# A two-layer graph network on one core: group sums laid between half batches, and two buffers for ScalarE's pair of passes

## The reference

```
# layer 0
msg = x[src] @ W_msg.T + b_msg + edge_embed[type]
messages = segment_sum(msg, dst, 3125)
x = layernorm(x + gru_cell(messages, x))
# layer 1, a SAGE layer applied twice (relu between)
neigh = segment_sum(h[src], dst) / max(degree, 1)
h = h @ w_self + neigh @ w_neigh + b
x = layernorm(x + h)
```

## Time and profile before

| | us |
|---|---|
| three runs | 766.2, 764.7, 766.98; median 766.2 |
| profiled execution: its time | 764.69 |
| its span, first to last instruction | 762.9 |
| time around the span (difference) | 1.8 |
| counting stage, first one-hot to the last pass of TensorE | about 15 to 403.6 |

### The profile page before, as it was taken

One profiled execution on the slowest core, in us unless ns is written; L12 is line 12 of the kernel. 1 busy time (PEld: TensorE's weight loads), 2 busy tenths in 40 slices (PEclk: granted clock), 3 DMA queues, 4 the chain that ended last, 5 costly groups with the idle time before them and its releaser, 6 DMA issues.

```text
span 762.9 us, 14609 instructions
## 1 busy us (share of the span) xinstructions
PE 662.5 (87%) x3061; PEld 311.9 (41%) x3061; DVE 468.4 (61%) x1469; ACT 244.3 (32%) x486; POOL 171.0 (22%) x342
## 2 busy tenths in 40 slices
PE   2767899989888899888766999948999999999995
PEld 0222344434333343333222544413555456666663
DVE  7789999998888879999894357651010010034434
ACT  3044444332422235656664245531111221100000
POOL 2432333232222235445340012230100111100000
PEclk9879999999999999999998999989999999999998
DMA  5000000000000000000002011000100110211210
GB/s 155 1 1 0 1 1 1 0 1 0 1 0 1 0 1 1 0 1 0 0 0 81 16 28 55 16 30 29 42 25 17 41 41 29 87 43 43 69 31 16
DMA packets 29437, 17.32 MB, mean 23 GB/s; under 512 B 1841, under 2 KB 28223, under 8 KB 29400
## 3 DMA queue, kind: packets, MB, share of 16 engines
q1 hardware_dynamic: 29400, 16.82, 7.6%
HBM read 10.38 MB, written 6.44 MB: 22 GB/s over the span
## 4 chain that ended last, share of the span: by engine, by line
PE 64%; DVE 18%; issue 7%; DVEq 5%; ACT 2%; DMA 1%; SPq 0%; POOL 0%; ACTq 0%
PE PS L917 14%; PE PS L994 11%; PE PS L1232 11%; PE PS L873 10%; DVE S L619 10%; DVE D L613 3%; PE PS L1161 3%; PE PS L1055 2%; PE PS L1196 2%; DVEq L619 2%; PE PS L895 1%; PE PS L1150 1%; PE PS L1149 1%; PE PS L1028 1%; PE PS L1029 1%
## 5 line engine op out<-in xcount | busy, mean ns | idle before, releaser
L917 PE MATMUL PS<-S,D 128*128 128x449 bf16 x780 | 219.0, 368 | 53.8 <-DVE S L619 45.4
L619 DVE TENSOR_SCALAR S<-iota_h,src_col,src_w 128x440 bf16<-128x440 f16 x749 | 253.1, 399 | 0.2 <-issue 0.2
L472 POOL COPY S<-T 128x27 bf16 (+1 forms) x262 | 113.5, 434 | 236.4 <-PE PS L917 222.2
L917 PEld LDWEIGHTS PS<-S,D 128*128 128x128 bf16 x780 | 75.7, 97 | 193.6 <-DVE S L619 152.3
L1275 ACT ACTIVATE AT<-digits 128x1152 uint8 (+5 forms) x75 | 77.1, 1029 | 160.7 <-DVE digits L608 160.7
L613 DVE TENSOR_TENSOR D<-iota_t,dst 128x384 bf16<-128x384 f16 x260 | 93.8, 361 | 33.3 <-PE PS L917 32.1
L873 PE MATMUL PS<-AT,xp 128*128 128x512 bf16 x375 | 91.3, 379 | 0.0
L994 PE MATMUL PS<-AT,x1p 128*128 (+2 forms) x450 | 86.8, 353 | 0.0
L1232 PE MATMUL PS<-xp,AT 128*128 128x384 bf16 (+1 forms) x525 | 85.6, 326 | 0.0
L1232 PEld LDWEIGHTS PS<-xp,AT 128*128 (+2 forms) x525 | 51.5, 98 | 33.9 <-issue 0.3
L994 PEld LDWEIGHTS PS<-AT,x1p 128*128 128x128 bf16 x450 | 39.5, 99 | 44.0 <-issue 2.3
(11 more groups left out here) (167 smaller groups left out, 628.8 us busy)
## 6 DMA issues: line engine op xcount, KB each, us to landing
slot<-x_rows SPq DMA_DIRECT2D x12, 256.0 KB, 2.9
xstage<-x SPq DMA_DIRECT2D x6, 256.0 KB, 4.9
x_rows<-slot SPq DMA_DIRECT2D x6, 256.0 KB, 2.2
y_rows<-slot SPq DMA_DIRECT2D x6, 256.0 KB, 2.2
res_rows<-slot SPq DMA_DIRECT2D x6, 256.0 KB, 2.2
slot<-res_rows SPq DMA_DIRECT2D x6, 256.0 KB, 3.1
out_rows<-slot SPq DMA_DIRECT2D x6, 256.0 KB, 2.2
slot<-xT SPq DMA_DIRECT2D x3, 256.0 KB, 2.6
```

What stands on the lines that cost most here:

```text
L472: g.tensor_copy(S[:, where:where + V, SPAN:WIDE], T[:, :, ds(c0 + where, V)].rearrange("p k c -> p c k")).then_inc(sem("types_placed"), 1)
L619: v.tensor_scalar(S[:, u, 0:SPAN], iota_h[:, :], src_col[:, ds(c0 + u, 1)], src_w[:, ds(c0 + u, 1)], ALU.is_equal, ALU.mult).then_inc(sem( ...
L917: mm(PS[:, par, 0:WIDE], ring[:, u, :], S[:, u, 0:WIDE], start=opens and u == 0, stop=last).then_inc(sem("tiles_summed" if last else "item ...
```

## The change

The plan of group sums is laid out for single steps. A table LEAST gives a least number of batches for each tile; that many passes, less one, are written out instead of looped, and a piece of steps stands after each of them and between its two halves. With `single = LEAST[t] - 2` there are `2 * single + 3` pieces: 3 in the tiles 0 to 8, 5 in 9 to 15, 7 in 16 to 18, 9 in 19 to 22, 23 in 23 and 24. The plan now sums to 125. The buffer `apart` becomes two buffers inside AT (a part that is written last), chosen by the parity of the batch, and ScalarE's wait after its second pass goes away. Four small table instructions of GpSimd at the start become ten.

```diff
--- before.py
+++ after.py
@@ -28,12 +28,11 @@
 TAIL = E - FULL * P
 U = 6
 V = U // 2
-PIECES = 3
 WIDE_TILES = 21
-LEAST = 2
-LEAST_WIDE = 4
+LEAST_RUNS = ((0, 9, 2), (9, 16, 3), (16, 19, 4), (19, 23, 5), (23, 25, 12))
+LEAST = tuple(n for lo, hi, n in LEAST_RUNS for _ in range(lo, hi))
 BATCHES = -(-CHUNKS // U)
-assert BATCHES < 1 << 10 and LEAST * WIDE_TILES + LEAST_WIDE * (TILES - WIDE_TILES) < BATCHES
+assert BATCHES < 1 << 10 and sum(LEAST) < BATCHES and len(LEAST) == TILES
 LAG = 3
 DIVIDE = -(-(1 << 16) // U)
 assert all(n * DIVIDE >> 16 == n // U for n in range(CHUNKS + U)) and (CHUNKS + U) * DIVIDE < 1 << 24
@@ -60,7 +59,7 @@
 CUTS = (0, 9, 18, TILES)
 EARLY = 5
 EARLY_BANKS = (2, 3, 5, 6, 7)
-EARLY_PLAN = (0,) * 7 + (4, 4, 5, 4, 5, 4, 5, 7, 5, 7, 7, 7, 8, 10, 9, 9, 10, 10)
+EARLY_PLAN = (0,) * 7 + (3, 3, 5, 3, 5, 3, 5, 6, 5, 6, 6, 6, 8, 9, 10, 11, 18, 13)
 EARLY_BEGIN = tuple(sum(EARLY_PLAN[:t]) for t in range(TILES + 1))
 assert EARLY_BEGIN[TILES] <= EARLY * TILES
 SCRATCH = 2048
@@ -104,6 +103,7 @@
 
 
     D_again = AT[:, TILES - 1 - U:TILES - 1, (TILES - 2) * P:(TILES - 1) * P]
+    apart = AT[:, 0:16, (TILES - 1) * P:(TILES - 1) * P + SPAN // 8]
     r = [A_at]
     digits = place(r, "digits", [P, WORDS, TURNED], i32)
     packedT = place(r, "packedT", [P, TURNED], i32)
@@ -181,7 +181,6 @@
     r = [Z_at]
     src_col = place(r, "src_col", [P, CP], fp32)
     src_w = place(r, "src_w", [P, CP], fp32)
-    apart = place(r, "apart", [P, SPAN], bf16)
     assert r[0] <= Z_at + 15 * F * 4
     emb_b = sb("emb_b", [NTYPE, F], fp32)
     gate_b = sb("gate_b", [F, 6], fp32)
@@ -440,11 +439,10 @@
             g.iota(iota_h[:, :], pattern=[[1, SPAN]], base=0, channel_multiplier=0, allow_small_or_imprecise_dtypes=True)
             g.iota(tile_off[:, :], pattern=[[P, TILES + 1]], base=-CENTER, channel_multiplier=0, allow_small_or_imprecise_dtypes=True)
             g.iota(thr[:, :], pattern=[[P, 1]], base=N - 1, channel_multiplier=-P, allow_small_or_imprecise_dtypes=True)
-            g.memset(least[:, 0:WIDE_TILES], LEAST)
-            g.memset(least[:, WIDE_TILES:TILES], LEAST_WIDE)
-            g.iota(plain[:, 0:WIDE_TILES], pattern=[[LEAST, WIDE_TILES]], base=1024 * LEAST, channel_multiplier=0, allow_small_or_imprecise_dtypes=True)
-            g.iota(plain[:, WIDE_TILES:TILES], pattern=[[LEAST_WIDE, TILES - WIDE_TILES]], base=1024 * LEAST_WIDE + LEAST * WIDE_TILES,
-                   channel_multiplier=0, allow_small_or_imprecise_dtypes=True)
+            for lo, hi, n in LEAST_RUNS:
+                g.memset(least[:, lo:hi], n)
+                g.iota(plain[:, lo:hi], pattern=[[n, hi - lo]], base=1024 * n + sum(LEAST[:lo]), channel_multiplier=0,
+                       allow_small_or_imprecise_dtypes=True)
             g.memset(at_i[:, TILES:TILES + 1], BATCHES - 1)
             g.memset(zero[:, :], 0.0)
             g.memset(ones[:, :], 1.0)
@@ -881,8 +879,7 @@
                     if j0 < j1:
                         early_sum(q, j0, j1)
 
-            def early_piece(t, n):
-                pieces = PIECES + 2 if is_dense(t) else PIECES
+            def early_piece(t, n, pieces):
                 n0, steps = EARLY_BEGIN[t], EARLY_PLAN[t]
                 early_steps(n0 + steps * n // pieces, n0 + steps * (n + 1) // pieces)
 
@@ -920,22 +917,18 @@
                 one_pass(first + t, None if t else 0, D_again, None, opens=True)
                 if t >= 2:
                     turn_tile(t - 2)
-                early_piece(t, 0)
-                if is_dense(t):
-                    for i in (1, 2):
-                        one_pass(first + t + i, first + i, D, None)
-                        early_piece(t, i)
-                    if t == TILES - 1:
+                single = LEAST[t] - 2
+                pieces = 2 * single + 3
+                early_piece(t, 0, pieces)
+                for i in range(1, single + 1):
+                    one_pass(first + t + i, first + i, D, i - 2 if is_dense(t) and i >= 3 else None, between_halves=lambda: early_piece(t, 2 * i - 1, pieces))
+                    early_piece(t, 2 * i, pieces)
+                    if t == TILES - 1 and i == 2:
                         turn_tile(t - 1)
-                    with pe.Fori(3, more) as i:
-                        one_pass(first + t + i, first + i, D, i - 2)
-                    early_piece(t, 3)
-                    one_pass(first + t + more, first + more, D, None, closes=True, between_halves=lambda: early_piece(t, 4))
-                else:
-                    with pe.Fori(1, more) as i:
-                        one_pass(first + t + i, first + i, D, None)
-                    early_piece(t, 1)
-                    one_pass(first + t + more, first + more, D, None, closes=True, between_halves=lambda: early_piece(t, 2))
+                with pe.Fori(single + 1, more) as i:
+                    one_pass(first + t + i, first + i, D, i - 2 if is_dense(t) else None)
+                early_piece(t, pieces - 2, pieces)
+                one_pass(first + t + more, first + more, D, None, closes=True, between_halves=lambda: early_piece(t, pieces - 1, pieces))
 
             pe.wait_ge(sem("entries_set"), 1)
             for t in range(TILES):
@@ -1297,11 +1290,14 @@
                 with act.Fori(3, more) as i:
                     b = first + i
                     c = first_chunk(b) + (U - 1)
-                    a.activation(apart[:, :], iota_h[:, :], ACT.Abs, scale=-1.0, bias=src_col[:, ds(c, 1)]).then_inc(sem(f"apart_set{t}"), 1)
+                    near = apart[:, ds((b & 1) * 8, 8), :]
+                    a.activation(near, iota_h[:, :].rearrange("p (a n) -> p a n", a=8), ACT.Abs, scale=-1.0,
+                                 bias=src_col[:, ds(c, 1)]).then_inc(sem(f"apart_set{t}"), 1)
                     act.wait_ge(sem(f"apart_set{t}"), i - 2)
                     act.wait_ge(sem("items_done"), items_until(t, b, 1))
-                    a.activation(S[:, U - 1, 0:SPAN], apart[:, :], ACT.Relu, scale=src_wn[:, ds(b.with_bounds(min_val=0, max_val=BATCHES), 1)], bias=src_w[:, ds(c, 1)]).then_inc(sem(f"S_last_set{t}"), 1)
-                    act.wait_ge(sem(f"S_last_set{t}"), i - 2)
+                    a.activation(S[:, U - 1, 0:SPAN].rearrange("p (a n) -> p a n", a=8), near, ACT.Relu,
+                                 scale=src_wn[:, ds(b.with_bounds(min_val=0, max_val=BATCHES), 1)],
+                                 bias=src_w[:, ds(c, 1)]).then_inc(sem(f"S_last_set{t}"), 1)
 
             def x_mid(c):
                 rows, k = (P, 4) if c < NC else (LAST, 1)
```

## The result

The changed kernel takes **740.11 us** (median of 4, 739.88 to 741.29) where the kernel before takes 766.59 (median of 4): a ratio of 0.9656, interval 0.9626 to 0.9686. The forecast was 741.3. The profiled execution took 740.08, its span is 738.3, so 24.6 us of span went.

What follows compares the result with a forecast made beforehand. VectorE was taken to pace the counting stage, stopped by TensorE's lumps of group sums. Terms -0.4 + 18.0 + 0.3 + 4.2 + 2.8 = 24.9 us, from 764.69, gave 739.8, or 741.3 against the median; range 736 to 751.

Steps and rivals of the forecast that it cites:

- Tiles 8 to 22: Counting stage: VectorE's idle 23.35 us shrinks to border waits of 4.5 and double steps of 0.9, gaining 18.0 us.
- Small stops inside tiles: Rival: a step inside each half batch still stops VectorE; some 115 pieces at 0.1 us give 753; chance 0.11.
- wrong if VectorE waits in the middle of tiles: Sign against the forecast in the counting stage: VectorE waiting inside tiles, not only at their borders; no size given.
- Tile 23: Next-to-last tile: idle 2.03 us less 1.25 at the border and 0.4 of TensorE's lag, gaining about 0.3 us.
- the ring: One batch of products between TensorE and VectorE; in tile 23 it hides about 0.7 of TensorE's 1.1 us lag.
- Tile 24: Last tile: 45.75 us falls to VectorE's work of 39.7 plus 1.8 for a stop and slow clock, gaining about 4.2.
- clock loss of 0.8: Tile 24: TensorE idles during VectorE's stop, then half speed for some 3 us costs 0.8 us more.
- the rival at 745: Tile 24: ScalarE's ring with TensorE, not the removed wait, makes the 2.33 us turn; 3.8 us don't come; chance 0.10.
- The clock in the stage: Rival, tiles 8 to 24: thinly spread bursts get TensorE half its clock, giving 808 us; chance 0.04.
- The end: Behind the last tile's passes: 15 products move into the tiles and `packed` comes 0.4 earlier, gaining 2.8 us.
- Straight code: TensorE's 37 more written-out passes: fetching their instructions taken as 0, with 8 us as upper bound.
- The start: GpSimd's six more table instructions delay VectorE's first operation and all that follows by 0.4 us.

Runs made afterwards that it cites:

- the plan alone: The changed kernel with one buffer and ScalarE's old wait behind its second pass: 743.9 us, ratio 0.9732 against the kernel before.
- straight code alone: Passes written out as in the changed kernel, but old numbers of steps at the old places and ScalarE's old pair: 764.89 us, ratio 1.0001 against the kernel before.
- in twos: The changed kernel with the step between the halves of a written-out batch moved behind the batch, so two stand together: 749.48 us, ratio 0.9807.
- entry early: The changed kernel, but TensorE reads the next tile's table entry ahead of the closing pass: 738.75 us, ratio 0.9664.
- help later: The changed kernel, but in tile 24 ScalarE's help begins at the fifth batch, not the fourth: 742.2 us, ratio 0.9709.
- five steps left: The changed kernel with 8 steps in tile 24 instead of 13, leaving five behind the last pass: 745.29 us, ratio 0.9749.
- all three: The changed kernel with table entry read early, tile 24's help a batch later and steps of tiles 14, 21, 22, 24 laid out anew: 738.06 us, ratio 0.9658.
- the zeros: Products of zeros on TensorE behind the last turn and the verdict's product, added to three kernels: changed 739.28, five steps left 741.45, all three 732.85 us.

## Why the prediction was right

**Tiles 8 to 22 (18.0, measured 16.6).** The mechanism is shown: the plan alone gives the same 206.90, straight code alone gives nothing, and the same steps in twos give back 3.06 there. The borders were forecast at 0.3 each, and most have 0.19 to 0.43. The price that was too low is that of the steps which still meet two by two in the tiles 14, 21 and 22: I put 0.9 by TensorE's work over VectorE's, but the borders into 21 and 22 have 0.77 and 0.63, and inside 21 and 22 stand 0.23, 0.88 and 0.24, 1.35 together. Waits for products make up most of the 7.03 us of idle time left; I had forecast 5.4 in all. The groups of line 871 are longer than three products at four places, as forecast (172.22, 279.90, 288.23 and 303.74); VectorE's waits from 97 us on are 11.0 us where about 9 were forecast.

**Small stops inside tiles** (the rival at 753) did not come where VectorE's half batch takes 1.18 us: from tile 8 to tile 20 the timeline has no wait but the border's, and the measured pitch of step and half batch is the predicted 1.22 us. They did come, small, in the helped batches, where one half takes 0.88. VectorE's timeline in tile 23 shows one bracket for it, 0.25 us at 318.01, but other starts of D are apart by more than the usual 0.88 with no bracket:

```profile
323.49 0.35 DVE L611 TENSOR_TENSOR D<-iota_t,dst 128x384 bf16<-128x384 f16 x1
324.36 0.36 DVE L611 TENSOR_TENSOR D<-iota_t,dst 128x384 bf16<-128x384 f16 x1
...
325.54 0.36 DVE L611 TENSOR_TENSOR D<-iota_t,dst 128x384 bf16<-128x384 f16 x1
326.65 0.36 DVE L611 TENSOR_TENSOR D<-iota_t,dst 128x384 bf16<-128x384 f16 x1
```

The first pair has 0.87, the second, of the same operations, 1.11. By the prediction's own sign ("wrong if VectorE waits in the middle of tiles") this is a partial miss. The kernel in twos pays more, 0.57 at a time.

**Tile 23** was forecast at a gain of 0.3 and lost 0.08. I let the ring hide 0.7 of TensorE's lag of 1.1. It hid none of it: the stretched half batches of this tile add up to 1.11 us, against 0.98 in before, while the border stayed what it was (1.87 us from the D_again pass to the first D, 1.91 before).

**Tile 24 (4.2, measured 3.99).** The prediction's working held in its largest place: ScalarE's first pass was put at 9.7 into the tile and started at 10.15, and the stop it causes, 1.0, was 1.31. The clock loss of 0.8 did not come. That 41.67 us are still close to the 41.5 of the forecast (39.7 + 1.8) is luck in part: 39.7 and 1.31 make 41.0, and the other 0.66 lies in places that the sum lacked, 0.29 of it in the first half batch (342.39 to 343.86, 1.47 where 1.18 is usual). These are the windows of after around that stop and across the helped batches:

```profile
350.00:352.00 2.00, 0.98 (x5) 0.29 (x3) 1.59 (x6) 1.19 (x3) 0.65 (x1) 1.00 0.02 4
354.00:376.00 22.00, 19.89 (x87) 7.83 (x85) 21.91 (x75) 15.34 (x23) 10.27 (x21) 1.00 0.00 1
```

ScalarE's turn is VectorE's 2.06. That the ring of ScalarE would hold it at 2.33 (the rival at 745) is refuted by its own timeline: when it catches up, its pairs follow at 1.73 us (353.25 to 354.98), and in the steady state it idles for TensorE, not for itself:

```profile
369.35 0.76 ACT L1298 ACTIVATE S<-AT,src_w,src_wn 128x440 bf16 x1 [0.41 <-PE PS L914]
370.18 0.67 ACT L1294 ACTIVATE AT<-iota_h,src_col 128x440 f16 x1
371.41 0.76 ACT L1298 ACTIVATE S<-AT,src_w,src_wn 128x440 bf16 x1 [0.57 <-PE PS L914]
```

**The clock in the stage** (the rival that ended slower, 808) stayed at 1.00 in all three windows of the tiles 8 to 24. The Trainium skill, "TensorE: Matmul & The Clock Gate", section "Part 1: The HAM clock gate", holds that full clock is earned by activity; the trace agrees so far: with TensorE busy for 19.89 of 22 us the granted clock stayed at 1.00.

**The end (2.8, measured 3.04)** came as worked out: `packed` at once when ScalarE is free, the turn behind it, only the date of the digits, 385.18, is 2 us later than the 383 forecast, since the stage gained 22.8 and the rest came behind it. The five left-over steps alone are 1.75 of the 3.04.

**Straight code** was priced at 0, and its kernel measures 1.0001. The Trainium skill, "Runtime: NRT & Kernel Launch", section "Instruction fetch mechanics", says that straight code is fetched ahead; three more packets moved, and the trace agrees that they were hidden.

**The start (-0.4, measured -0.92).** The tables took 0.40: VectorE's first operation starts at 3.72 and not 3.32. The rest is not theirs, as the kernel with passes written out shows (14.92): in the changed kernel VectorE waited for ScalarE's copy of the sources, which came from a later transfer.

**What the sum did not have** is the stretch behind the verdict, +1.79. I had taken all that comes after the stage as untouched. By instructions it is; by TensorE's clock it is not. That the total came within 1.2 us of the forecast is in part luck: this gain made up for the tiles 8 to 22, which gave 1.4 less. It lies between the layers, where before takes 7.68 us for the 27 products and the changed kernel 5.99, which is 1.69 less. Five other kernels with steps placed after the new plan (in twos, entry early, help later, five steps left, all three) have 7.16 to 7.68 there, so it is not a gain that the change secures.

## What to carry to other kernels

Where one engine sets the pace through a short ring, filler work for the other is cheap when it is cut to the grain of the ring: here one group per half batch was free at 1.22 against 1.18 us and cost about 1 us in a tile whose half batches go down to 0.88, while the same groups in pairs cost 7.9 us. When a stage gets shorter and the program does not, compare the granted clock behind the stage before doubting the gain; a few products of zeros in TensorE's idle gap are a cheap test of it, and here gave back 4.1 us at that place. A second buffer and the removal of its wait are one edit: with the wait left in, the buffers made tile 24 slower by 2 us, by their address work as far as the code tells.

## What the runs showed of the hardware that I had not expected

- After an idle time of 4.2 us TensorE was granted about half its clock (0.50 to 0.59 over 6 us) in all eleven kernels without the zeros. In the second 6 us it had 0.98 to 1.00 in four of them and 0.50 to 0.67 in seven. Over all kernels the same instructions behind the verdict took 348.32 to 354.71 us.
- Between the layers the same 27 products took 5.99 us or up to 7.68, by whether the half clock fell on them or on products that TensorE has time for.
- Reading a table entry into TensorE's registers at a border held a light tile back by 0.27 to 0.45 us (9.03 against 8.76 and 8.58), though no engine shows as busy with it.
- About 0.15 us of idle time on ScalarE's queue, put down to address work, stood on the critical path once per batch in one kernel; in the changed kernel ScalarE idles for TensorE instead.
